# A pipelined middle stage on one Trainium2 core: PSUM banks of the down results and the ranks, place of the LayerNorm, order of the sync queue

## The reference, cut to what matters

```
h = signature_features(x) @ W.T + b                       # truncated signature, depth 4, 8 channels
# lambda layer on LN(h)
q, v = batchnorm(LN(h) @ Wq + bq), batchnorm(LN(h) @ Wv + bv)
k = softmax over time of (LN(h) @ Wk + bk)
lam_c = einsum('bukt,buvt->bkv', k, v)                    # content lambda
lam_p = relu(conv3x3(v, Wpos))                            # position lambda
Y = einsum('bhkt,bkv->bhvt', q, lam_c) + einsum('bhkt,bkvt->bhvt', q, lam_p)
h = h + Y @ Wout + bout
# feed-forward on x = LN(h): top-1 of 8 experts plus a shared expert
y = w2[e] @ (silu(w1[e] x) * (w3[e] x)) for the expert e with the largest gate logit
h = h + y + gelu(x @ sw1.T) @ sw2.T
```

## Time and profile before

| | us |
|---|---|
| median of 3 runs | 728.63 |
| the runs | 727.95, 732.63, 728.63 |
| the profiled execution | 722.27 |
| its span, first to last instruction | 720.5 |

### The profile page before, as it was taken

One profiled execution on the slowest core, in us unless ns is written; L12 is line 12 of the kernel. 1 busy time (PEld: TensorE's weight loads), 2 busy tenths in 40 slices (PEclk: granted clock), 3 DMA queues, 4 the chain that ended last, 5 costly groups with the idle time before them and its releaser, 6 DMA issues. The chain is left out here.

```text
span 720.5 us, 13466 instructions
## 1 busy us (share of the span) xinstructions
PE 615.8 (85%) x3740; PEld 490.5 (68%) x3740; DVE 499.2 (69%) x1381; ACT 280.3 (39%) x691; POOL 301.4 (42%) x303
## 2 busy tenths in 40 slices
PE   3789999999999999824988878888988629999995
PEld 1568888888888888613666655666666517888884
DVE  6888899999998888662476555646657325777774
ACT  4233233333333232112374454644554404555552
POOL 4734244555554332011164656545554521333333
PEclk9899999999999999955699977989889757999998
DMA  9004666666654455553213223223221112222220
GB/s 273 0 1 151 181 181 186 199 199 197 194 165 153 150 160 170 188 116 117 94 57 88 88 88 104 75 87 91 72 83 38 30 57 54 73 62 70 74 57 9
DMA packets 88227, 79.89 MB, mean 111 GB/s; under 512 B 27798, under 2 KB 81133, under 8 KB 87030
## 3 DMA queue, kind: packets, MB, share of 16 engines
q1 hardware_dynamic: 84886, 73.06, 34.1%
q0 software_dynamic: 3296, 6.27, 2.8%
HBM read 31.76 MB, written 48.09 MB: 111 GB/s over the span
## 5 line engine op out<-in xcount | busy, mean ns | idle before, releaser
L1015 DVE SCALAR_TENSOR_TENSOR P<-PS,QN 128x512 f32<-128x512 f32 x128 | 79.3, 682 | 47.0 <-PE PS L1134 47.0
L523 DVE SCALAR_TENSOR_TENSOR Z<-PS,Vt,Z 126x128 f32<-126x128 f32 x224 | 78.7, 351 | 8.4 <-PE PS L644 0.6
L644 PE MATMUL PS<-Wh,Ah 128*126 128x512 f32 x256 | 78.4, 429 | 0.0
L1288 POOL DMA_INDIRECT out_h<-OS,XS x39 | 37.9, 971 | 92.2 <-DVE OS L1332 91.8
L644 PE MATMUL PS<-Wl,Ah 128*126 128x512 f32 x256 | 70.4, 397 | 2.2 <-DVE Wl L487 2.2
L313 POOL TENSOR_TENSOR INCl<-INC,INCh 126x512 fp32r<-126x512 f32 x31 | 40.1, 1293 | 74.5 <-ACT INCh L390 74.5
L644 PE MATMUL PS<-Wh,Al 128*126 128x512 f32 x256 | 71.2, 400 | 0.0
L644 PEld LDWEIGHTS PS<-Wl,Ah 128*126 128x126 f32 x256 | 47.9, 187 | 14.7 <-issue 2.7
L644 PEld LDWEIGHTS PS<-Wh,Al 128*126 128x126 f32 x256 | 48.4, 189 | 12.5
L871 POOL TENSOR_TENSOR Gl<-GF,Gh 128x504 fp32r<-128x504 f32 x32 | 39.5, 1254 | 32.3 <-ACT GF L922 32.3
L430 ACT ACTIVATE XT<-PS 128x126 f32<-128x126 f32 x32 | 8.9, 277 | 107.3 <-PE PS L690 107.3
(11 more groups left out here) (224 smaller groups left out, 1642.8 us busy)
## 6 DMA issues: line engine op xcount, KB each, us to landing
routed<-nobody SPq DMA_DIRECT2D x30, 1170.0 KB, 5.4
IM<-v_pad SPq DMA_DIRECT2D x128, 78.8 KB
XS<-routed SPq DMA_DIRECT2D x39, 130.0 KB, 2.1
WRW<-in_w SPq DMA_DIRECT2D x16, 256.0 KB, 3.2
R<-h_rows SPq DMA_DIRECT2D x16, 129.9 KB
W1l<-in_wsig SPq DMA_DIRECT2D x4, 512.0 KB, 7.4
WR<-in_w SPq DMA_DIRECT2D x8, 256.0 KB, 2.9
q_raw<-QS SPq DMA_DIRECT2D x32, 63.0 KB
```

Source lines behind the costliest of these rows:

```text
L523: ins = dve.scalar_tensor_tensor(Z[:, u], psU[h][:, d], sc, Z[:, u], ALU.mult, ALU.add)
L644: ins = pe.matmul(out, a, w, start=(n == 0), stop=(n == len(turn) - 1))
L1015: ins = dve.scalar_tensor_tensor(P[:, b, HV * h:HV * h + HV], psC[2 * pair + hb], 0.0, QN[:, g % 2, b:b + 1].broadcast_to([128, HV, SP]), ...
L1288: pool.indirect_dma_start(out_rows, bass.IndirectOffsetOnAxis(XS[:, k % XB, IDC:IDC + 1].bitcast(i32), 0), OS[:, k % 2], None, bounds_chec ...
```

## The change

It leaves the arithmetic and the number of instructions alone and changes banks, orders and waits:

- psF moves from bank 6 to bank 4 (psU, first half), psR from bank 7 to bank 5 (psU, second half).
- TensorE: `up(g)` now waits for the down addition of group g-1 (bs_ready) and for the positions of the last pair (pos_ready); `down` no longer waits for yc_ready, psY no longer for bs_ready, psL and the last psH no longer for pos_ready. `rank` moves from behind `up` to behind `down`, ahead of `conv(k, 3)`, and no longer waits for the logits' copy.
- DVE: reciprocal and scaling (LayerNorm) move ahead of the two down additions; `place` moves ahead of products(k, 2) and (k, 3).
- SyncE: load_im(k+2) comes first in the step, then load_q, load_w2, and last the wait for the scatter with load_h.

```diff
@@ -779,12 +779,12 @@
         psC = [PS[n][:, :].rearrange("p (v s) -> p v s", v=HV) for n in range(4)]
         psU = [PS[4 + h][:, 0:2 * CT].rearrange("p (i s) -> p i s", i=2) for h in range(2)]
         psY = PS[6][:, 0:GB * SP].rearrange("p (b s) -> p b s", b=GB)
-        psF = PS[6][0:TOK, :].rearrange("p (t h f) -> p t h f", t=2, h=2)
+        psF = PS[4][0:TOK, :].rearrange("p (t h f) -> p t h f", t=2, h=2)
         psH = PS[7][0:TOK, 0:2 * F].rearrange("p (t f) -> p t f", t=2)
         psX = PS[7][:, 0:CT]
         psG = PS[7][0:TOK, 0:2 * E].rearrange("p (t e) -> p t e", t=2)
         psL = PS[7][:, 0:GB * DK].rearrange("p (b v) -> p b v", b=GB)
-        psR = PS[7][0:TOK, 0:4 * E].rearrange("p (t e) -> p t e", t=4)
+        psR = PS[5][0:TOK, 0:4 * E].rearrange("p (t e) -> p t e", t=4)
         psN = PS[7][0:1, 0:E]
         psV = PS[7][0:2 * NB, 0:2 * DK].rearrange("p (c k) -> p c k", c=2)
 
@@ -834,17 +834,17 @@
             load_im(1)
             for k in range(NG):
                 if on(k + 2, 0, NG):
+                    sp.wait_ge(conv_done, 4 * k + 4)
+                    load_im(k + 2)
                     sp.wait_ge(qn_ready, k + 1)
                     load_q(k + 2)
-                    if k + 2 >= RB:
-                        sp.wait_ge(scattered[(k + 2) % RB], 32 * ((k + 2) // RB))
-                    load_h(k + 2)
                 if on(k, 2, E):
                     sp.wait_ge(w2_lo, k - 1)
                     load_w2(k)
                 if on(k + 2, 0, NG):
-                    sp.wait_ge(conv_done, 4 * k + 4)
-                    load_im(k + 2)
+                    if k + 2 >= RB:
+                        sp.wait_ge(scattered[(k + 2) % RB], 32 * ((k + 2) // RB))
+                    load_h(k + 2)
 
         @block.gpsimd
         def _(pool):
@@ -1059,11 +1059,6 @@
                     dve.memset(carrier[:], 0.0)
                     for t in range(2):
                         dve.bn_aggr(MV[:, u, t], ST[:, u, t]).then_inc(mv_ready, 1)
-                if on(f, 0, NG):
-                    dve.wait_ge(down_done, f + 1)
-                    base = rows(f, HC, ROW)
-                    L.link(dve.tensor_tensor(base, psF[:, :, 0], base, ALU.add))
-                    dve.tensor_tensor(base, psF[:, :, 1], base, ALU.add).then_inc(bs_ready, 1)
                 if on(g, 0, NG):
                     dve.wait_ge(sd_ready, g + 1)
                     L.link(dve.reciprocal(SD[:, u, :, 1], SD[:, u, :, 0]))
@@ -1073,12 +1068,17 @@
                         if t == 0:
                             L.made(ins)
                     ins.then_inc(xn_ready, 1)
+                if on(f, 0, NG):
+                    dve.wait_ge(down_done, f + 1)
+                    base = rows(f, HC, ROW)
+                    L.link(dve.tensor_tensor(base, psF[:, :, 0], base, ALU.add))
+                    dve.tensor_tensor(base, psF[:, :, 1], base, ALU.add).then_inc(bs_ready, 1)
+                if k % 2 and on((k - 3) // 2, 0, NM):
+                    place((k - 3) // 2)
                 if on(k, 0, NG):
                     wait_from_one(dve, sum_done, 2 * k)
                     products(k, 2)
                     products(k, 3)
-                if k % 2 and on((k - 3) // 2, 0, NM):
-                    place((k - 3) // 2)
                 if k % 2 == 0 and on((k - 2) // 2, 0, NM):
                     choose((k - 2) // 2)
             for k in range(NG + 2):
@@ -1147,6 +1147,8 @@
             def up(g):
 
                 pe.wait_ge(xl_ready, g + 1)
+                wait_from_one(pe, bs_ready, g)
+                wait_from_one(pe, pos_ready, g // 2)
                 wait_from_one(pe, gf_ready, 2 * g)
                 for i in range(IC):
                     for n, (a, x) in enumerate(((S1h, X2h), (S1l, X2h), (S1h, X2l))):
@@ -1157,8 +1159,6 @@
             def down(g):
 
                 pe.wait_ge(gl_ready, 2 * g + 2)
-                if on(g + 1, 0, NG):
-                    pe.wait_ge(yc_ready, g + 2)
                 for t in range(2):
                     for i in range(IC):
                         for n, a in enumerate((Gh, Gl)):
@@ -1189,20 +1189,19 @@
 
                     pe.wait_ge(yc_ready, g + 1)
                     pe.wait_ge(ls_ready, min(k + 1, NG))
-                    if k == NG:
-                        pe.wait_ge(pos_ready, (k - 4) // 2 + 1)
                     for t in range(2):
                         ins = pe.matmul(psH[:, t], YC[:, g % 2, 2 * t:2 * t + 2].rearrange("p b s -> p (b s)"), WO[:], start=True, stop=True)
                     ins.then_inc(ht_done, 1)
                 if on(f, 0, NG):
                     down(f)
+                if k % 2 and on((k - 3) // 2, 0, NM):
+                    rank((k - 3) // 2)
                 if on(k, 0, NG):
                     conv(k, 3)
 
                     pe.wait_ge(lc_ready, k + 1)
                     pe.wait_ge(qn_ready, k + 1)
                     wait_from_one(pe, yc_ready, k)
-                    wait_from_one(pe, bs_ready, k - 1)
                     for b in range(GB):
                         ins = pe.matmul(psY[:, b], LC[:, k % 2, DK * b:DK * b + DK].rearrange("p v h -> p (v h)"), QN[:, k % 2, b],
                                         start=(b == 0), stop=False)
@@ -1222,17 +1221,11 @@
                         ins = pe.matmul(psG[:, t], XG[:, g % 2, TOK * t:TOK * t + TOK], GW[:], start=True, stop=True)
                     ins.then_inc(gate_done, 1)
                     up(g)
-                if k % 2 and on((k - 3) // 2, 0, NM):
-                    if on(g, 0, NG):
-                        pe.wait_ge(lg_ready, g + 1)
-                    rank((k - 3) // 2)
                 if on(k + 1, 0, NG):
 
                     pe.wait_ge(kh_ready, k + 2)
                     if on(g, 0, NG):
                         pe.wait_ge(lg_ready, g + 1)
-                    if k % 2 and k >= 3:
-                        pe.wait_ge(pos_ready, (k - 3) // 2 + 1)
                     for b in range(GB):
                         ins = pe.matmul(psL[:, b], KH[:, w, b].rearrange("p h k -> p (h k)"), VT[:, (k + 1) * GB + b].rearrange("p j r -> p (j r)"), start=True, stop=True)
                     ins.then_inc(lam_done, 1)
```

## The result

| | before | after |
|---|---|---|
| median us | 729.45 (4 runs, 727.95 to 732.63) | 707.03 (4 runs, 702.35 to 709.80) |
| profiled execution, its span | 722.27, 720.5 | 709.80, 708.0 |
| ratio to before, 95% interval | | 0.9692 (0.9634 to 0.975) |

703 had been predicted, with a range of 697 to 717. The two profiles differ by less (12.5 us) than the medians (22.4), since the profiled execution of before was a quick one and that of after the slowest of its four.

A forecast was written before the change was run, and what follows sets the result against it. TensorE's chain through the middle stage's loop was taken as the bound. Loop 201.2 to 174.3 us (27.0 less), end 1.9, minus 1.5 for queries and 2 for the clock: 25.4 off 728.63 gives 703 us, range 697 to 717.

The forecast's parts named there:

- L1207's 0.64: TensorE, middle loop: with down results in the up product's bank, L1207 stops waiting for DVE's addition, 0.64 us in 14 steps.
- the positions' 0.80: TensorE, odd steps: ranking ahead of the last convolution removes L1237's 0.80 us wait for positions, with no new one.
- the LayerNorm that must move with the bank: DVE: normalised rows at 6.4 us of the step instead of 8.2, ahead of transposes wanted at 7.88; leaves 1.4 us.
- `up`'s new waits: TensorE: `up` waits for the previous group's additions, done by 7.5, and positions, about 8.3; needed near 10 and 11, no cost.
- The end: End of the loop: about 0.95 us won at L1195's wait for positions, another 0.95 at the transposes, 1.9 in all.
- Queries: Sync queue: load_q behind eight V-row issues lands 12.3 to 13.4 us after the first; cost 0 to 6 us, 1.5 taken.
- The rival: Queries land late, 15.5 us after the first V-row issue; about 16 us on top of 699.7 gives 716; chance 0.11.
- Clock: TensorE, loop: waits ahead of today's slow stretches go; 2 us left for stretches at 1.2 GHz.
- V rows first: Sync queue: V rows issued when the last convolution ends, two steps ahead of need; the 6.3 us of L1134 waits go.
- Clock on the path: TensorE, loop: the clock still falls after the short rank matmuls, 6.9 to 20.3 us, giving 713; chance 0.17.
- L1071 held: DVE: L1071 held so long beside GpSimd that transposes wait instead, 9.0 us lost, 709; chance 0.06.
- Slower: TensorE at 1.2 GHz for most of the loop, more than 72 us of 174; 90 us gives 745; chance 0.04.

The follow-up runs named there:

- queries first: The changed kernel with load_q(k+2) issued ahead of load_im(k+2) on the sync queue; 695.33 us, ratio 0.9563.
- the LayerNorm's: The changed kernel with load_q ahead of load_im, and the down additions put back ahead of the LayerNorm; 708.74 us, ratio 0.9658.
- V rows first alone: The kernel before with only the sync queue's new order; 725.19 us, ratio 0.9914.
- the doubled ranking: The changed kernel with load_q ahead of load_im, and the rank matmuls issued twice in their new place; 724.0 us, ratio 0.9915.
- loop's-start profile: The changed kernel with load_q ahead of load_im, and load_h(1), load_w2(0), load_w2(1) issued behind the first V rows; 697.65 us, ratio 0.9549.

## Why the prediction was right, and where it was not

| | predicted | after | queries first |
|---|---|---|---|
| even step | 11.98 | 11.93 + X2l wait | 11.93 |
| odd step | 13.05 | 12.97, two + X2l wait | 12.96 |
| step 2 | 11.98 | 13.50 | 14.03 |
| last step | 12.10 | 12.37 | 12.38 |
| loop, step 2 to its end | 174.3 | 185.9 | 175.8 |
| from there to the first expert | 31.7 | 31.2 | 31.6 |

(The loop of the changed kernel runs from 364.38 to 550.32, that of the queries-first kernel from 362.45 to 538.20.)

*Steps of the sum.* The two step lengths are right to 0.1 us: L1207's 0.64, the positions' 0.80, the LayerNorm that must move with the bank, the rank matmuls at equal cost in their new place, `up`'s new waits hidden. (A ranking is ten matmuls in the trace, five instructions of two passes, not the eight told ahead of the prediction; its 1.07 us holds.) The end gave 2.4 for 1.9. The gross sum of 174.3 is what the queries-first kernel does (175.8), with step 2 its only real excess.

*Queries: the step that failed.* 1.5 us were allowed; TensorE stood 7.65 us in eight waits on X2l. Two parts were wrong. The estimate of 12.3 to 13.4 us from the first V-row issue to the landing was taken near its lower end, while 5.8 of issues and a median landing of 7.7 make 13.5, and the steps took 13.1 to 14.2. The prediction's own figure for the upper end, 6 us in the even steps, is what came: 6.5 in six of them. And "it does not hold that back" was false. load_h was timed by the old kernel's scatter, at 16.4 us after the start of step 4, ahead of an issue at 19. The scatter was issued at the same place in the new order (13.5 us after the start of step 5, 13.3 in the old row), but with V rows streaming beside it took 7.5 us to land instead of 3.0, and its load_h left at 21.0, 1.0 us after the V rows could have gone. This happened in four steps; the two odd steps with a stand (9 and 11) came behind such a one. The rival had the mechanism and priced it at 16 us; it came at 9 to 12.

*Clock.* 2 us were allowed. In the changed kernel the one stretch in mid-loop cost 0.7 us in step 6 and 2.35 in step 7, 3.1 in all. Step 2 cost 1.5 more than a clean one, because TensorE stayed at 1.2 GHz until 371.3 us, not until 356.5 as in the profile of before. In all eleven other profiles of this study the clock was low from 356.5 to 366, in those with the old sync order or the old ranking too (in one, the LayerNorm's, it had risen at 348 and fell again at 355). So the early rise was most likely a matter of that one execution, on which the sum was built; a second profile of before would settle it and was not taken. The predicted span was 695.1 us, the measured one is 708.0. Of the 12.9 between them, step 2 begins 5.3 later than in the earlier trace rows (first stage and slow clock), the loop behind it is 8.1 longer than 174.3 + 1.5 + 2, and the end gives 0.5 more. By the medians only 4 us are missing, and that is in part luck: the sum was made on a profile 6.4 us quicker than the median of its kernel, and the changed kernel's profile was 2.8 slower than its own.

*What is worth what.* The text gave the rank move 0.80 x 6 + 0.95 = 5.8 us and left the slow stretches to a term of their own. In the runs the two are one: 13 us. The bank move was given 0.64 x 14 = 9.0; it is worth about 6, all in even steps, once the ranking covers it in odd ones. V rows first alone measured what it was given, 6.3 us by the ratio of 0.9914 (2.6 to 9.8 by its interval), though its profiled loop is only 0.7 us shorter than that of before; and it decided whether the rest was worth anything.

*Rivals.* Clock on the path: one stretch, 3.1 us, in this kernel and not behind a ranking; the doubled ranking shows the mechanism to be real with twice the matmuls. L1071 held: it came true where it did no harm. Two scalings (now L1066) took 0.60 us in the changed kernel. In the queries-first kernel, where GpSimd makes the queries at the same time, they take 1.02 us in seven steps and up to 1.36 in five, and the even steps stay at 11.93. Slower: nothing of it.

## What to carry to other kernels

A list of waits on one engine is not a list of gains. Of four edits, the order of one DMA queue decided whether shorter steps were possible at all, and the rank move gave twice its wait, since slow clock came with the old place too. When a queue's order changes, time again every transfer that now runs beside others, and whatever is issued on its landing: here the scatter's landing had been measured with no V rows beside it. Put a small load with little room ahead of a bundle with two steps of room.

## What the runs showed of the hardware

A stand of 0.80 us between the ten short matmuls of a ranking and Lambda's eight was followed by 6 to 7 us at 1.2 GHz in all six places; twenty short matmuls without a stand, by 13.5 us in three of six. A stand of 0.67 us ahead of down, between long matmuls, occurs in every step at the full clock, and in the queries-first loop none of them was followed by a slow stretch; in the loop's-start profile, with the same loop code, one in step 8 was (1.0 us later, for some 7 us). Which of idle time and small matmuls the clock answers to, and in what sum, these runs leave open.

Vector work was held up beside GpSimd work. In the changed kernel's VectorE timeline around 427 us, beside GpSimd's X2l and weight part, two operations of 0.19 us took:

```profile
427.39 0.65 DVE L1027 TENSOR_TENSOR eq<-eq,K 126x32 f32<-126x32 f32 x1
...
428.29 1.00 DVE L1029 TENSOR_TENSOR OH<-K,top 126x32 f32<-126x32 f32 x1
...
L1029 DVE TENSOR_TENSOR OH<-K,top x8: 191/192/997, 377.4 to 558.6; 126x32 f32<-126x32 f32 x8
```

The last row gives a line's min/median/max in ns. The Trainium skill, "SBUF — State Buffer", Who interferes with whom, says that a VectorE instruction with two SBUF inputs contends with a GpSimd instruction that reads SBUF; the trace agrees (1.00 against 0.19), though no wait of TensorE in this trace is put down to these operations.
